# Attention scores from six part products, on 64 rows of TensorE each, beside the transposed scores, with value products spread over four heads

## The reference

```python
def _L0_attn_ref(x, w_qkv, w_proj):
    DIM, NHEAD, WINDOW = (128, 16, 128)
    DK = DIM // NHEAD
    ...
    q, k, v = (heads(q), heads(k), heads(v))
    attn = jnp.einsum('bhqd,bhkd->bhqk', q, k) / math.sqrt(DK)
    mask = jnp.abs(idx[None, :] - idx[:, None]) > WINDOW
    attn = jnp.where(mask[None, None], -1000000000.0, attn)
    p = jax.nn.softmax(attn, axis=-1)
    out = jnp.einsum('bhqk,bhkd->bhqd', p, v)
    ...
x = x + _L0_attn_ref(_layernorm(x, axis=-1), L0_attn_w_qkv, L0_attn_w_proj)
x = x + _L0_ffn_ref(_layernorm(x, axis=-1), ...)
```

## Time and profile before

| | |
|---|---|
| median of 3 runs | 1817.72 us (1816.0 to 1820.92) |
| the profiled execution's own time | 1817.61 us |
| its span, first to last instruction | 1815.9 us |
| attention (to about 760 us) and ffn (the rest) | some 760 and 1056 us |
| PE, DVE, ACT, POOL busy over the span | 85%, 82%, 70%, 73% |

### The profile page before, as it was taken

How to read it: one execution, slowest core, us unless ns; L and a number is a source line. 1 busy time by engine, 2 the same in 40 slices (tenths; PEclk the granted TensorE clock), 3 DMA queues, 4 the chain that set the end, 5 groups by cost and what they waited for, 6 DMA issues and landing times.

```text
span 1815.9 us, 37722 instructions
## 1 busy us (share of the span) xinstructions
PE 1536.1 (85%) x11712; PEld 1091.8 (60%) x11712; DVE 1481.7 (82%) x3720; ACT 1268.6 (70%) x1741; POOL 1332.3 (73%) x1579
## 2 busy tenths in 40 slices
PE   3899999999999999768887888878878788887877
PEld 2455555555556666346666766666666666666656
DVE  3668888788888887159899988989889898898988
ACT  1156666666666666558888878888888888788885
POOL 1045555555555555569999999999999999999993
PEclk9689999999999999879999998999999999999999
DMA  5334444443444442100000000000000000000000
GB/s 141 76 81 98 99 97 95 101 96 95 103 103 103 99 99 56 43 29 1 19 18 1 19 18 18 0 18 18 1 18 18 11 8 18 18 0 18 13 6 7
DMA packets 73406, 85.14 MB, mean 47 GB/s; under 512 B 9856, under 2 KB 63616, under 8 KB 68608
## 3 DMA queue, kind: packets, MB, share of 16 engines
q1 hardware_dynamic: 73312, 84.08, 19.7%
HBM read 58.10 MB, written 25.95 MB: 46 GB/s over the span
## 4 chain that ended last, share of the span: by engine, by line
POOL 24%; issue 19%; DVE 7%; ACT 5%; PE 1%; POOLq 0%; DVEq 0%; ACTq 0%; SPq 0%
POOL SUM L751 24%; DVE W L944 4%; ACT E L852 3%; ACT L786 1%; DVE M8Y L888 0%; PE WT L1012 0%; DVE SMALL L888 0%; DVE SMALL L905 0%; ACT GE L785 0%; DVE CT L927 0%; ACT SIM L779 0%; ACT BNT L794 0%; PE MB L979 0%; DVE Z L911 0%; PE E L967 0%
## 5 line engine op out<-in xcount | busy, mean ns | idle before, releaser
L751 POOL TENSOR_TENSOR SUM<-SIM 128x1024 f32<-128x1024 f32 x512 | 959.9, 1912 | 39.8 <-DVE W L944 36.1
L944 DVE SCALAR_TENSOR_TENSOR W<-SUM,SMALL,E 128x1024 f32<-128x1024 f32 x512 | 646.1, 1280 | 86.2 <-ACT E L852 82.1
L852 ACT ACTIVATE E<-SUM,NB 128x1024 f32<-128x1024 f32 x512 | 567.4, 1118 | 136.1 <-DVE W L944 121.6
L1012 PE MATMUL WT<-idf,W 128*128 128x128 f32 x4096 | 554.3, 285 | 104.2 <-DVE CT L927 53.5
L1012 PEld LDWEIGHTS WT<-idf,W 128*128 128x128 f32 x4096 | 476.3, 147 | 274.8 <-DVE W L944 143.0
L264 POOL TENSOR_SCALAR_AFFINE_SELECT PT<-PT 128x128 f32<-128x128 f32 (+1 forms) x1024 | 336.4, 353 | 323.4 <-ACT PT L354 287.2
L409 DVE TENSOR_REDUCE mx<-SX 128x2 f32<-128x512 f32 x256 | 175.4, 685 | 102.7 <-PE SX L492 102.0
L411 DVE TENSOR_REDUCE mx<-SY 128x2 f32<-128x768 f32 x256 | 242.7, 948 | 7.7 <-PE SY L492 7.3
L354 ACT ACTIVATE PT<-TX 128x512 f32<-128x512 f32 x256 | 152.8, 597 | 102.2 <-PE TX L519 100.9
L356 ACT ACTIVATE PT<-TY 128x768 f32<-128x768 f32 x256 | 207.0, 808 | 2.0 <-PE TY L519 0.8
L488 PE MATMUL SY<-K,Q 72*128 72x384 bf16 x512 | 164.0, 343 | 15.6 <-DVE mx L411 14.9
(11 more groups left out here) (111 smaller groups left out, 1671.1 us busy)
## 6 DMA issues: line engine op xcount, KB each, us to landing
K<-k_parts SPq DMA_DIRECT2D x96, 192.0 KB
Q<-q_parts SPq DMA_DIRECT2D x288, 64.0 KB
q_parts<-qp SPq DMA_DIRECT2D x16, 384.0 KB, 2.4
k_parts<-kp SPq DMA_DIRECT2D x16, 384.0 KB, 2.4
xin<-in_x SPq DMA_DIRECT2D x16, 256.0 KB, 3.1
xres<-in_x SPq DMA_DIRECT2D x16, 256.0 KB, 9.0
x<-X SPq DMA_DIRECT2D x16, 256.0 KB, 2.3
x2T<-X2T SPq DMA_DIRECT2D x16, 256.0 KB, 2.1
```

Of the source, the lines that this page charges most:

```text
L751: return eng.tensor_tensor(SUM[(q * FH + h) % RING][:, :].rearrange("p (i j) -> p i j", i=NK), sx, sy, ALU.add)
L852: nc.scalar.activation(E[h % 2][:, :], SUM[(k * FH + h) % RING][:, :], ACT.Exp, bias=NB[q][:, h:h + 1]).then_inc(S["exp_ready"], 1)
L944: nc.vector.scalar_tensor_tensor(out=W[h % WRING][:, :], in0=SUM[(k * FH + h) % RING][:, :], scalar=TOP[q][:, h, TOPK - 1:TOPK], in1=E[h % ...
L1012: o = pe.matmul(WT[:, e, :], W[h % WRING][:, e * P:(e + 1) * P], ident[:, :], is_transpose=True, start=(h == 0 and e % 4 == 0), stop=(h == ...
```

## The change

Three products of parts are left out of nine: `TERMS` pairs part 0 with three parts, part 1 with two, part 2 with one, so that a score takes 48 rows. The rows are loaded twice, at rows 0 and at rows 64 (`HALF`), in both `Q` and `K`. Scores run on rows 0 to 47 (query tile 2 on rows 64 to 111), transposed scores on rows 64 to 114. One function `heads` issues both in turns. Identity and band are cut into two halves of 64 rows, so a band mask takes two products.

```diff
-            for a in range(3):
-                sp.dma_start(K[b][24 * a:24 * a + 24, hs, :],
-                             k_parts.rearrange("a (d h) n -> (a d) h n", h=H)[:, hs, :]).then_inc(to, 16)
-                for e in range(3):
-                    r = 24 * a + 8 * e
-                    sp.dma_start(Q[b][r:r + 8, hs, :],
-                                 q_parts[a].rearrange("(d h) n -> d h n", h=H)[:, hs, :]).then_inc(to, 16)
+            for r in (0, HALF):
+                for e, n in TERMS:
+                    sp.dma_start(K[b][r:r + DK * n, hs, :],
+                                 k_parts[0:n].rearrange("a (d h) n -> (a d) h n", h=H)[:, hs, :]).then_inc(to, 16)
+                    for a in range(n):
+                        sp.dma_start(Q[b][r + DK * a:r + DK * a + DK, hs, :],
+                                     q_parts[e].rearrange("(d h) n -> d h n", h=H)[:, hs, :]).then_inc(to, 16)
+                    r += DK * n
...
+        def heads(t, c, h):
...
+            if scoresT and h == 0:
+                pe.wait_ge(S["max_rows_loaded"], 32 * (t - 1) + 16)
+            if scoresT and h == 8:
+                pe.wait_ge(S["max_rows_loaded"], 32 * (t - 1) + 32)
+
+            sx = SX[:, :, :].rearrange("p j n -> p (j n)")
+            if scores:
+                if c > 0 or h > 0:
+                    pe.wait_ge(S["outer_maxima"], n - 1)
+                tile(SX[:, 0, :], 0, 0, 0, 2)
```

More of the change, by code:

```diff
@@ L40 @@
 EPS = 1e-5
-TERMS = 9
-KQ = TERMS * DK
+TERMS = ((0, 3), (1, 2), (2, 1))
+KQ = DK * sum(n for _, n in TERMS)
 SHIFT = 3
+HALF = P // 2
+LOADS = 16 * 2 * sum(1 + n for _, n in TERMS)
 HT = H // 2 * TILES
@@ L282, in step @@
                     mask(y[:, :, 256:384], True, False).then_inc(S["exp_masked"], 1)
[L284 removed]
+                if h == 14 and 0 <= c - 2 < SEQS:
                     pool.wait_ge(S["x1_variance"], t - 1)
@@ L532, in _, with values @@
         SPAN = [(0, 0, 2), (512, 0, 3), (896, 1, 4), (256, 2, 4)]
-        def values(s, c, g):
+        def values(s, c, g, j):
             b = c % 2
-            pe.wait_ge(S["exp_masked"], (s * H + 4 * g + 4) * 4)
-            if g == 0:
+            if j == 0:
+                pe.wait_ge(S["exp_masked"], (s * H + 4 * g + 4) * 4)
+            if j == 0 and g == 0:
                 pe.wait_ge(S["v_ready"], s + 1)
-            if g % 2 == 0 and (c > 0 or g > 0):
+            if j == 0 and g % 2 == 0 and (c > 0 or g > 0):
@@ L541, in values @@
                 pe.wait_ge(S["values_copied"], s * 2 + g // 2)
-            for j, (at, q0, q1) in enumerate(SPAN):
-                for e in range(4):
-                    h, slot = 4 * g + e, g % 2 * VSUB + (j * 8 + g // 2 * 4 + e) * SLOT_V
-                    o = pe.matmul(PV[32 * e:32 * e + 32, q0 * P:q1 * P], V[b][:, slot:slot + SLOT_V],
-                                  PT[:, h % 8, at:at + (q1 - q0) * P], start=(j == 0 and g % 2 == 0), stop=(j == 3 and g % 2 == 1),
-                                  skip_group_check=True)
@@ L548, in values @@
-            o.then_inc(S["values_product"], 1)
+            at, q0, q1 = SPAN[j]
+            for e in range(4):
+                h, slot = 4 * g + e, g % 2 * VSUB + (j * 8 + g // 2 * 4 + e) * SLOT_V
+                o = pe.matmul(PV[32 * e:32 * e + 32, q0 * P:q1 * P], V[b][:, slot:slot + SLOT_V],
+                              PT[:, h % 8, at:at + (q1 - q0) * P], start=(j == 0 and g % 2 == 0), stop=(j == 3 and g % 2 == 1),
+                              skip_group_check=True)
+            if j == 3:
+                o.then_inc(S["values_product"], 1)
@@ L552, in step @@
             for h in range(H):
-                if 0 <= c < SEQS:
-                    scores(t, c, h)
+                heads(t, c, h)
                 if h == 1 and 0 <= c - 1 < SEQS:
@@ L620, in step @@
                 for g, (sl, ds_) in enumerate(VSLOT):
-                    if h == sl and 0 <= c - ds_ < SEQS:
-                        values(t - ds_, c - ds_, g)
-                if 0 <= c - 1 < SEQS:
-                    scoresT(t, c, h)
+                    if sl <= h < sl + 4 and 0 <= c - ds_ < SEQS:
+                        values(t - ds_, c - ds_, g, h - sl)
         steps(pe, step)
@@ L1054 @@
     keep = np.arange(P)[None, :] >= np.arange(P)[:, None]
+    high, low = np.where(keep.T, 0, -1e30), np.where(keep, 0, -1e30)
+    band = np.concatenate([high, low, high], axis=1)
     arrays = {
```

237 lines of the change are left out of this document (129 added, 108 removed), and 2 rows, old and new, of the table SHARED.

## The result

The changed kernel takes 1980.78 us (median of 4 runs, 1964.86 to 1992.68), the kernel before 1816.93 us beside it: a ratio of 1.089, 95% interval 1.081 to 1.097. The prediction was 1967 us, 1855 to 2035, with 0.89 on slower. The profiled execution of the changed kernel took 1980.06 us.

What follows compares the result with a forecast made beforehand. The prediction took a chain through DRAM, already as long as the 43.1 us step, as the bound. Its terms made a step of 53.5 us; over 14 steps plus edges about 149 us onto 1817.6, 1967 us, range 1855 to 2035.

Steps and rivals of the forecast that it cites:

- the chain through DRAM: In attention, k's third part through stores and loads to the next step's maxima: already as long as the 43.1 us step.
- B: Part of a step from k's store to the load of the maxima: predicted 16.8 us plus 3.5 for added rows.
- C: Part of a step from the load of the maxima to the next step's first reduction: predicted 3.2 us.
- A: Part from a step's first reduction to k's third part's end: predicted 27.6 us plus 2.4 for the clock, 24.0 before.
- Pairs of products: On PE, products on both row halves overlap: a head 0.93 us instead of 1.43, net 5.6 us off a step.
- To the reduction of head 4, then the walk: 10.7 + 16.9: Step start to head 4's reduction 10.7 us, then serial waits between DVE and PE through MB to k's end, 16.9.
- the term for the clock: PE at 1.2 GHz after idling at a step's end: about 1.5 heads slowed, 2.4 us a step.
- The middle, 16.8 + 3.5: From k's store to the load of the maxima: 16.8 us as today, 3.5 more for 192 rows instead of 144.
- From the load to the next reduction, 3.2: From the issue of the maxima's load to the next step's first reduction: 3.2 us.
- The edges: Outside the 14 chain steps: first heads' rows 3.5 us later, step 15 may win 1 or 2, last two left.
- the shorter walk: Rival: shorter walk through MB, clock stays up; 25.2 us to k's end, step 48.7, total 1838 to 1900; chance 0.24.
- The other side: Rival: transfers stay hidden, engines bind, PE's saving counts; step about 38.5 us, 64 us less, 1753 us; chance 0.08.

Runs made afterwards that it cites:

- a_fewer: Changed kernel without the second band product of a head's scores, 64 TensorE instructions less in a loop body of two steps: 1963.6 us, ratio 1.082.
- a_filler: Changed kernel with four unneeded float32 products on PE ahead of its wait for the maxima at head 0: 2008.4 us, ratio 1.108.
- a_144rows: Changed kernel with the transfers of before, 144 rows in 12 issues, without the loads of Q into rows 0 to 47: 1923.8 us, ratio 1.060.
- a_wide: Changed kernel with the same 192 rows loaded in 4 transfers of 48 rows, q and k stored in 9 stores: 1922.4 us, ratio 1.062.
- b_192rows: Kernel before with the transfers alone, six more 8-row loads of Q that no product reads, 192 rows in 18 issues: 1884.5 us, ratio 1.038.
- a_wide_vf_between: Changed kernel with 4 wide row loads, value products ahead of the jobs on MB, and the maxima's store between the row loads: 1869.7 us, ratio 1.029.

## Why the prediction was right

The reason given was that the chain through DRAM sets the step and that what relieves PE does not show. The first half was shown: the transfers alone make the kernel before slower by 4.4 us a step, and the changed kernel gets faster with fewer rows, faster rows, or a shorter walk. Of the second half there is one sign, in the changed kernel: a_fewer takes 64 TensorE instructions out of two steps, and the step falls by 0.4 us. No run relieved PE in the kernel before and left the rest as it was, so that part stays open. The 9.7 us by which the step grew are 4.6 in B, 1.0 in C, 2.1 for the new order in A at the full clock, and 1.9 for the clock in A. By the prediction's terms:

- *Pairs of products.* Right: they start at the same time (372.90), and a head of both kinds streams in some 0.9 us. PE's busy time in 13 steps stayed at 522 us all the same, since 122 us of it fell into stretches at 1.2 GHz. With these counted at half, the work is 61 us less, 4.7 a step by this estimate, where a net 5.6 was predicted.
- *To the reduction of head 4, then the walk: 10.7 + 16.9.* The changed kernel has, in DVE's timeline:

```profile
358.80 0.69 DVE L466 TENSOR_REDUCE mx<-SX 128x2 f32<-128x512 f32 x1 [5.41 <-PE SX L517]
...
368.73 0.68 DVE L466 TENSOR_REDUCE mx<-SX 128x2 f32<-128x512 f32 x1
...
376.81 0.69 DVE L466 TENSOR_REDUCE mx<-SX 128x2 f32<-128x512 f32 x1 [1.17 <-PE SX L517]
...
381.25 0.69 DVE L466 TENSOR_REDUCE mx<-SX 128x2 f32<-128x512 f32 x1 [1.42 <-PE SX L517]
...
384.96 0.68 DVE L434 TENSOR_TENSOR kp<-rk,kp 128x512 bf16<-128x512 f32 x1
```

  Head 4 comes 9.9 us into this step (10.8 in the mean), and k's third part ends at 385.64, 16.9 behind it (17.2 in the mean). The reductions of heads 7 and 8, shown here, wait 1.17 and 1.42 us for SX, as the walk said, and that of head 9 starts 26.7 us into a step in the mean, where "some 26 us or more" was the sign. With the term for the clock A was to be 30.0 and was 28.0. Steps at the full clock (those of a_filler, and the ones of a_144rows and a_wide named above) have 9.3 to head 4 and 16.8 from there: the walk was right to 0.1 us, the way to head 4 was put 1.4 too long, and the clock 0.5 too dear.
- *The middle, 16.8 + 3.5.* 21.2 instead of 20.3. The rows added are worth 3.1 by b_192rows and 3.5 by a_144rows, as predicted; B grew by 4.6. What the last 1.1 to 1.5 us are stays open; it is not the fetches, without which B is 21.6. The test that was named, 13.6 us for 192 rows against 12 or less, came out as 13.8 in b_192rows and 15.6 in the changed kernel. Expected were 9 to 10 us between the first load's issue and the store of the maxima; it is 6.8, which is 18 issues of 0.38, near the 0.33 that the prediction itself took for one. No term hung on it.
- *From the load to the next reduction, 3.2.* 3.5.
- *Sum.* 52.8 a step instead of 53.5. PE's first wait by total is at head 0 for `m_parts`, as named, but 32.0 us in some 12 steps (9 waits, 3.6 in the mean) instead of 6 a step; DVE's idle time there is 5.3 in the mean of steps 3 to 15.
- *The edges* were mis-sized: 14 steps of 9.5 (1 to 14) make 132.5 instead of 146, while the rest came to 29.9 instead of 3. The first scores wait 17.8 us instead of 11.0, twice the 3.5 added; step 0 takes 6.2 more; and steps 15 and 16, of which 15 was to gain 1 or 2 us, take 14.8 more. In these two the mean clock is 0.71, against 0.93 before, and head 8 of step 15 waits 6.6 us for its maxima. That 1967 is so close to 1981 is in part luck: the two errors, 13.5 us too much in the steps and 27 too little at the edges, have opposite signs.

Of the rivals, the shorter walk was the nearest: it put A at 25.2 with the clock up, and at the full clock A is 26.1. But the clock did not stay up, so its 48.7 a step did not come. The other side, where transfers stay hidden, needed B at 16.8 and A under 22.5; the changed kernel has neither, and no version of it has A under 25.9.

## What to carry to other kernels

Before relieving the busiest engine, add up the longest chain that has to close once in a step, its DMA landings and the waits between engines: at 93% busy TensorE was not alone in setting this step, for 3.1 us more in the chain made it 4.4 us longer. Where a chain through DRAM is that long, transfer time is kernel time, and the shape of a transfer (48 rows at once, not 8) is worth more than its bytes. An idle stretch in the chain can cost twice, since the clock is low behind it: compare only steps with the same granted clock before blaming the order of the code. And when code grows in a loop, look at the page's row of the instruction queue: 36 packets became 78 here when the body had grown past some size.

## What the hardware showed that I had not expected

- A loop body that grew from some 1601 to 1663 TensorE instructions was fetched again in each turn, 78 packets of 16 KB against 36. Taking 64 out stopped it (42). Where the transfer engines were at 0.99, PE stood for 5.5 us (6.1 in a_wide_vf_between); the queue's share of the span (0.3%) tells nothing of it.
- The same 192 rows need 18.1 us from the first load to the load of the maxima in 18 transfers, and 12.9 in 4 (means of steps 3 to 13; 144 rows in 12 transfers before: 13.5). A store of 24 KB behind them pays for it in full.
- One wait of 7.0 us with every engine idle cost a second time: PE then worked at 1.2 GHz for the next 3.3 us. All in all the lower clock costs 1.9 us a step in the changed kernel, and 3.1 in b_192rows, where no product was changed.
